# A transformer kernel on one core: the mixture layer's base matmuls first, its low-rank terms stacked, its second router joined to the output

## The reference

```python
# x: 1024 tokens x 128; W1 128x512, W2 512x128; E = 3 experts of rank R = 8
gates = softmax(x @ Rw)                                    # per token, 3 values
base  = x @ W + b
z     = einsum('bsd,edr->ebsr', x, A)                      # 3 x 8 values per token
zg    = z * gates
out   = base + (1 / 8) * einsum('ebsr,erh->bsh', zg, Bm)
...
h = relu(_mole(x, W1, b1, A1, B1, R1))
out = _mole(h, W2, b2, A2, B2, R2)
```

## Time and profile before

| what | value |
|---|---|
| runs, median (lowest to highest of 3) | 780.85 us (779.65 to 781.73) |
| span of the profiled execution | 780.1 us |
| PE busy in it | 706.0 us (90%) |
| DVE, ACT, POOL busy | 435.9, 316.3, 109.9 us |
| mixture layer, first router matmul to first expert matmul | 108.17 to 162.26 us of the span |

### The profile page before, as it was taken

One profiled execution on the slowest core, in us unless ns is written; L12 is line 12 of the kernel. 1 busy time (PEld: TensorE's weight loads), 2 busy tenths in 40 slices (PEclk: granted clock), 3 DMA queues, 4 the chain that ended last, 5 costly groups with the idle time before them and its releaser, 6 DMA issues.

```text
span 780.1 us, 9898 instructions
## 1 busy us (share of the span) xinstructions
PE 706.0 (90%) x3509; PEld 473.5 (61%) x3509; DVE 435.9 (56%) x1028; ACT 316.3 (41%) x501; POOL 109.9 (14%) x88
## 2 busy tenths in 40 slices
PE   9976999999999679999999999999977998999996
PEld 5655584878876345555555555555555885655585
DVE  5579220145575746666666666666645467534444
ACT  3044102035442345555555555555532542054441
POOL 0120030003310001111111111111132360200000
PEclk9599869699997779999999999999996998699998
DMA  3111863000004000101010101010000000000000
GB/s 79 29 44 43 243 167 80 1 1 0 1 1 134 0 1 1 41 1 42 0 41 0 41 0 42 0 41 0 0 1 1 1 1 0 1 0 1 0 1 28
DMA packets 43347, 21.62 MB, mean 28 GB/s; under 512 B 14347, under 2 KB 40469, under 8 KB 43312
## 3 DMA queue, kind: packets, MB, share of 16 engines
q1 hardware_dynamic: 43312, 21.16, 10.1%
HBM read 20.55 MB, written 0.52 MB: 27 GB/s over the span
## 4 chain that ended last, share of the span: by engine, by line
PE 54%; issue 28%; DVE 11%; POOL 5%; ACT 2%; POOLq 0%; DVEq 0%
PE ps L1347 8%; PE ps L1362 8%; PE ps L1153 6%; POOL rstd L481 5%; PE ps L1565 5%; PE ps L1581 4%; PE ps L1146 2%; PE ps L1587 2%; PE ps L1199 2%; PE ps L1456 1%; PE ps L1313 1%; PE ps L1444 1%; PE ps L1280 1%; PE ps L1322 1%; DVE z L942 1%
## 5 line engine op out<-in xcount | busy, mean ns | idle before, releaser
L1153 PE MATMUL ps<-filler 128*128 128x512 bf16 x382 | 107.2, 426 | 1.5 <-POOL filler L468 0.9
L481 POOL TENSOR_TENSOR rstd<-rv,minus_half 128x4 f32<-128x4 f32 x34 | 46.9, 1380 | 349.8 <-DVE rv L795 349.8
L952 DVE SCALAR_TENSOR_TENSOR zr<-ps,zr 128x512 fp32r<-128x512 f32 x96 | 65.1, 690 | 54.5 <-ACT zr L630 54.3
L630 ACT ACTIVATE zr<-ps 128x512 fp32r<-128x512 f32 x96 | 57.5, 599 | 69.1 <-PE ps L1347 65.1
L1456 PE MATMUL ps<-wl,z 128*128 128x128 f32 x512 | 69.2, 285 | 5.2 <-ACT z L685 5.2
L1444 PE MATMUL ps<-cf,wl 128*128 128x512 f32 x128 | 63.5, 619 | 7.0 <-ACT cf L548 7.0
L1456 PEld LDWEIGHTS ps<-wl,z 128*128 128x128 f32 x512 | 62.0, 195 | 11.6 <-ACT z L685 7.9
L1153 PEld LDWEIGHTS ps<-filler 128*128 128x128 bf16 x382 | 40.4, 108 | 43.5 <-issue 15.2
L1347 PE MATMUL ps<-zr 128*128 128x512 f32 x192 | 62.2, 406 | 1.5 <-DVE zr L928 1.5
L1110 DVE SCALAR_TENSOR_TENSOR z<-z,kc 128x512 f32<-128x512 f32 x48 | 34.7, 751 | 47.8 <-ACT z L745 47.8
L1362 PE MATMUL ps<-zr 128*128 128x512 f32 x192 | 59.4, 390 | 2.0 <-DVE zr L952 2.0
(11 more groups left out here) (249 smaller groups left out, 1180.1 us busy)
## 6 DMA issues: line engine op xcount, KB each, us to landing
wl<-in_L_attn_W SPq DMA_DIRECT2D x16, 256.0 KB
big<-in_L_cond_weight SPq DMA_DIRECT2D x32, 64.0 KB, 1.8
arena<-in_L_cond_expert_wi SPq DMA_DIRECT2D x1, 1024.0 KB, 9.1
arena<-in_L_cond_expert_wo SPq DMA_DIRECT2D x4, 256.0 KB, 5.8
big<-in_L_ffn_q_w SPq DMA_DIRECT2D x2, 512.0 KB
big<-in_L_ffn_k_w SPq DMA_DIRECT2D x2, 512.0 KB
tree_v<-in_L_ffn_v_w SPq DMA_DIRECT2D x2, 512.0 KB
arena<-in_L_cond_share_wi SPq DMA_DIRECT2D x1, 768.0 KB, 5.6
```

Source lines behind the costliest of these rows:

```text
L481: nc.gpsimd.tensor_tensor(rstd[:, half, :], rv[:, half, :], minus_half[:, :], ALU.pow).then_inc(S_["rstd"], 1)
L630: nc.scalar.activation(hidden_part(h, n, 0), ps[h][:, n % 2, :], ACT.Relu).then_inc(S_[k + "_hi"], 1)
L952: V.scalar_tensor_tensor(hidden_part(h, n, 1), ps[h][:, n % 2, :], 0.0, hidden_part(h, n, 0), ALU.max, ALU.subtract).then_inc(S_[k + "_lo" ...
L1153: T.matmul(bank, filler[:, :].to_broadcast([P, P]), filler[:, :].to_broadcast([P, HT]), start=True, stop=True)
```

## The change

First linear: after the router's matmuls (now in bank 3) PE runs six of the eight base matmuls (chunks 0 to 2 of both halves, `base_in`) without a filler, then the transposes, and then adds the low-rank terms into the same banks; chunk 3's base matmul stands just ahead of its low-rank one. Low-rank terms: `zg` holds three copies of the 25 columns side by side in blocks of 32, so that one transpose gives 96 rows. ACT's copy rounds these to fp32r; DVE then replaces rows 32 to 63 by the remainder (`low_part`, a new step with the new wait `d_zl` on PE). The weights are stacked likewise in `lora_r`: rounded, rounded, remainder. One fp32r matmul over 96 rows then gives high x high + low x high + high x low. Second linear: `w2f` carries 155 columns (128 of W2 and 27 of A2, R2), so each hidden tile is used by one matmul for both (`base_out`, into banks 0 and 1, 256 columns per tile); the low-rank terms are added later (`lora_out`). The second round goes half by half: DVE does all of half 0, then all of half 1, then both residual sums. The fillers of `turn_parts` are gone; six stand ahead of half 1's turn. The loads of B1, b1, B2, b2 are made three times (12 instead of 4); POOL clears `zg` and makes `lora_r` ahead of the experts' split. The gate vectors' softmax starts ahead of the first mixture. Ten semaphores of the set-up become two counters (`p_mm`, `p_mmc`) with the same order; their lines are left out of the diff, and so are most removed lines, which stand in the listing above.

```diff
-        ar2 = sb("ar2", [P, FC, MER + ME])
-        b1aug = sb("b1aug", [MER + 1, FF])
-        b2aug = sb("b2aug", [MER + 1, D])
+        lora_r = sb("lora_r", [3 * QUAD, FF + D], F32R)
         w1f = sb("w1f", [P, FF])
-        w2f = sb("w2f", [P, FC, D])
+        w2f = sb("w2f", [P, FC, D + MER + ME])
...
-        zg = sb("zg", [P, 2, TILES, QUAD])
-        zgt = sb("zgt", [QUAD, 2, HT])
+        zgt = sb("zgt", [3 * QUAD, 2, HT], F32R)
...
+        lora = selt[:, :, :].rearrange("p h n -> p (h n)")[:, 0:FF + D]
+        zg = [Z[h][:, 10, 0:TILES * P].rearrange("p (i r k) -> p i r k", i=TILES, r=P // QUAD) for h in HALVES]
...
+        def second_out(h):
+            return ps[h][:, 0:2, :].rearrange("p b (i n) -> p (b i) n", i=TILES // 2)
...
+                load(w2f[:, :, D + e * MR:D + (e + 1) * MR], I["L0_ffn_A2"][e].rearrange("(c p) r -> p c r", p=P), "ld_d")
             load(ar1[:, MER:MER + ME], I["L0_ffn_R1"], "ld_d")
-            load(ar2[:, :, MER:MER + ME], I["L0_ffn_R2"].rearrange("(c p) e -> p c e", p=P), "ld_d")
+            load(w2f[:, :, D + MER:D + MER + ME], I["L0_ffn_R2"].rearrange("(c p) e -> p c e", p=P), "ld_d")
+            sp.wait_ge(S_["k_mem"], 7)
+            for r in range(0, 3 * QUAD, QUAD):
+                load(lora[r:r + MER, 0:FF], I["L0_ffn_B1"].rearrange("e r n -> (e r) n"), "ld_d")
+                load(lora[r + MER:r + MER + 1, 0:FF], row("L0_ffn_b1"), "ld_d")
+                load(lora[r:r + MER, FF:], I["L0_ffn_B2"].rearrange("e r n -> (e r) n"), "ld_d")
+                load(lora[r + MER:r + MER + 1, FF:], row("L0_ffn_b2"), "ld_d")
             load(w1f[:, :], I["L0_ffn_W1"], "ld_d")
-            load(w2f[:, :, :], I["L0_ffn_W2"].rearrange("(c p) n -> p c n", p=P), "ld_d")
+            load(w2f[:, :, 0:D], I["L0_ffn_W2"].rearrange("(c p) n -> p c n", p=P), "ld_d")
...
+            for h in HALVES:
+                own.link(nc.gpsimd.memset(zg[h], 0.0))
+                nc.gpsimd.memset(zg[h][:, :, 0:3, MER:MER + 1], 1.0).then_inc(S_["d_zi"], 1)
+            pool.wait_ge(S_["ld_d"], 16 * (2 * ME + 16))
+            own.link(nc.gpsimd.tensor_copy(lora_r[:, :], lora[:, :]))
+            low = slice(2 * QUAD, 3 * QUAD)
+            nc.gpsimd.tensor_tensor(lora_r[low, :], lora[low, :], lora_r[low, :], ALU.subtract).then_inc(S_["d_w"], 1)
+            pool.wait_ge(S_["d_w"], 1)
...
             act.wait_ge(S_["p_gw"], 1)
             nc.scalar.activation(gvec[:, 1, :], gvec[:, 1, :], ACT.Exp, scale=10.0,
                                  accum_out=gred[:, 1:2]).then_inc(S_["p_gw"], 1)
+            def mixture_exp(r, h):
+                act.wait_ge(S_["d_z"], 5 + 2 * h if r else 1 + h)
+                nc.scalar.activation(logit[:, h], logit[:, h], ACT.Exp).then_inc(S_["d_e"], 1)
+            def mixture_out(r, h):
+                act.wait_ge(S_["d_zt"], 2 * r + h + 1)
+                copy(zgt[:, h], ps[h][0:3 * QUAD, 3, :], "d_ztc")
+            for h in HALVES:
+                mixture_exp(0, h)
+            for h in HALVES:
+                mixture_out(0, h)
+            for h in HALVES:
+                for c in range(FC):
+                    act.wait_ge(S_["d_hid"], h * FC + c + 1)
+                    nc.scalar.activation(z(h, c), ps[h][:, c, :], ACT.Relu).then_inc(S_["d_relu"], 1)
+            for h in HALVES:
+                mixture_exp(1, h)
+                mixture_out(1, h)
...
+            dve.wait_ge(S_["ld_gv"], 16)
+            own.link(V.tensor_reduce(gred[:, 0:1], gvec[:, 0, :], AX_X, ALU.max))
+            V.tensor_scalar(gvec[:, 1, :], gvec[:, 0, :], gred[:, 0:1], None, ALU.subtract).then_inc(S_["p_gw"], 1)
             def mixture(r):
-                zr = [ps[h][:, (1, 0)[r], :].rearrange("p (i k) -> p i k", i=TILES) for h in HALVES]
+                zr = [second_out(h)[:, :, D:] if r else ps[h][:, 3, :].rearrange("p (i k) -> p i k", i=TILES) for h in HALVES]
+                rest = slice(QUAD, 2 * QUAD)
+                def logits(h):
                     dve.wait_ge(S_[("d_r1", "d_r2")[r]], h + 1)
                     own.link(V.tensor_reduce(small[:, h, 0:TILES], zr[h][:, :, MER:MER + ME], AX_X, ALU.max))
                     V.tensor_tensor(logit[:, h], zr[h][:, :, MER:MER + ME], spread(small[:, h, 0:TILES], ME), ALU.subtract
                                     ).then_inc(S_["d_z"], 1)
+                def weighted(h):
                     dve.wait_ge(S_["d_e"], 2 * r + h + 1)
                     own.link(V.tensor_reduce(small[:, h, 4:4 + TILES], logit[:, h], AX_X, ALU.add))
                     own.link(V.reciprocal(small[:, h, 8:8 + TILES], small[:, h, 4:4 + TILES]))
                                                     spread(small[:, h, 8:8 + TILES], ME), ALU.mult, ALU.mult))
                     if r == 1:
                         dve.wait_ge(S_["d_zt"], h + 1)
-                    V.tensor_tensor(zg[:, h, :, 0:MER].rearrange("p i (e r) -> p i e r", e=ME),
-                                    zr[h][:, :, 0:MER].rearrange("p i (e r) -> p i e r", e=ME),
-                                    spread(logit[:, h], MR), ALU.mult).then_inc(S_["d_z"], 1)
-            dve.wait_ge(S_["k_mem"], 8)
+                    own.link(V.tensor_tensor(zg[h][:, :, 0, 0:MER].rearrange("p i (e r) -> p i e r", e=ME),
+                                             zr[h][:, :, 0:MER].rearrange("p i (e r) -> p i e r", e=ME),
+                                             spread(logit[:, h], MR), ALU.mult))
+                    V.tensor_copy(zg[h][:, :, 1:3, 0:MER], zg[h][:, :, 0:1, 0:MER].to_broadcast([P, TILES, 2, MER])
+                                  ).then_inc(S_["d_z"], 1)
+                def low_part(h):
+                    dve.wait_ge(S_["d_ztc"], 2 * r + h + 1)
+                    V.tensor_tensor(zgt[rest, h], ps[h][rest, 3, :], zgt[rest, h], ALU.subtract).then_inc(S_["d_zl"], 1)
+                if r == 0:
+                    for h in HALVES:
+                        logits(h)
+                    for h in HALVES:
+                        weighted(h)
+                    for h in HALVES:
+                        low_part(h)
+                else:
+                    for h in HALVES:
+                        logits(h)
+                        weighted(h)
+                        low_part(h)
+            dve.wait_ge(S_["d_zi"], 2)
...
-                residual(h, ps[h][:, 1, :], xt[1], xt[0], "d_res")
+                V.tensor_tensor(xt[0][:, h], second_out(h)[:, :, 0:D], xt[1][:, h], ALU.add).then_inc(S_["d_res"], 1)
...
-            pe.wait_ge(S_["ld_d"], 16 * (2 * ME + 8))
+            pe.wait_ge(S_["ld_d"], 16 * (2 * ME + 16))
             for h in HALVES:
                 pe.wait_ge(S_["c_out"], h + 1)
                 for i in range(TILES):
+                    ins = T.matmul(ps[h][:, 3, i * P:i * P + MER + ME], cf[:, h][:, tok(h, i)], ar1[:, :], start=True, stop=True)
                 ins.then_inc(S_["d_r1"], 1)
-            def turn_parts(r):
-                keep_warm(4, ps[0][:, 2, :])
+            def base_in(c, h):
+                T.matmul(ps[h][:, c, :], w1f[:, c * P:(c + 1) * P], cf[:, h], start=True, stop=False)
+            def turn_parts(r, h):
+                pe.wait_ge(S_["d_z"], 6 + 2 * h if r else 3 + h)
+                for i in range(TILES):
+                    ins = T.transpose(ps[h][0:3 * QUAD, 3, tok(h, i)], zg[h][:, i, 0:3].rearrange("p r k -> p (r k)"), ident)
+                ins.then_inc(S_["d_zt"], 1)
+            for c in range(FC - 1):
+                for h in HALVES:
+                    base_in(c, h)
+            for h in HALVES:
+                turn_parts(0, h)
+            pe.wait_ge(S_["d_w"], 1)
+            for h in HALVES:
+                pe.wait_ge(S_["d_zl"], h + 1)
+                for c in range(FC):
+                    if c == FC - 1:
+                        base_in(c, h)
+                    T.matmul(ps[h][:, c, :], lora_r[:, c * P:(c + 1) * P], zgt[:, h], start=False, stop=True
                              ).then_inc(S_["d_hid"], 1)
+            def base_out(h, tiles):
+                for i in tiles:
+                    for c in range(FC):
+                        ins = T.matmul(second_out(h)[:, i, 0:D + MER + ME], z(h, c)[:, tok(h, i)], w2f[:, c, :],
+                                       start=(i % 2 == 0 and c == 0), stop=False, skip_group_check=True)
+                if TILES - 1 in tiles:
+                    ins.then_inc(S_["d_r2"], 1)
+            def lora_out(h):
+                pe.wait_ge(S_["d_zl"], 2 + h + 1)
                 for i in range(TILES):
-                for i in range(TILES):
+                    ins = T.matmul(second_out(h)[:, i, 0:D], zgt[:, h, tok(h, i)], lora_r[:, FF:],
+                                   start=False, stop=True, skip_group_check=True)
                 ins.then_inc(S_["d_out"], 1)
+            pe.wait_ge(S_["d_relu"], FC)
+            base_out(0, range(TILES))
+            pe.wait_ge(S_["d_relu"], 2 * FC)
+            base_out(1, range(TILES // 2))
```

(8 more changed lines are left out.)

114 lines of the change are left out of this document (33 added, 81 removed).

## The result

The changed kernel took 755.95 us (median of 4 runs, 754.89 to 760.88), the kernel before 781.29 us beside it (779.65 to 790.66). The ratio is 0.970, with a 95% interval of 0.967 to 0.974: some 23 us faster. The forecast was 761.3 us, with a range of 758.5 to 767.0.

A forecast was written before the change was run, and what follows sets the result against it. The mixture stage was taken as bound by TensorE's work and its clock. Stage terms gave 162.26 - 142.7 = 19.6 us, so span 780.1 becomes 760.5, plus 0.75 makes 761.3 us; range 758.5 to 767.0.

The forecast's parts named there:

- The sum of the new stage: Router to first expert matmul: that matmul moves from 162.26 to 142.7 us, a gain of 19.6 us.
- six base matmuls: First linear: start near 111.6 us, 1.7 us each at low clock until 114.5, then 0.893 each, ending at 118.35.
- The wait d_zl: First linear, after the stack's transposes: TensorE waits for VectorE's low part from 119.45 to 120.45 us.
- changes of row count: First linear's low-rank and last base matmuls: four changes at 0.15 us each, 0.6 us in all.
- The joined matmul: Second linear: 155 columns at 0.294 us each, 32 taking 9.4 us; bounds 0.249 and 0.473.
- the tail: Half 1's turn to experts: grows, TensorE nearly idle from 137.85 to 142; 0.55 us added for low-clock transposes.
- Loads, GpSimd, renamed semaphores: Eight more load issues cost 2.9 us, GpSimd's split starts near 101.4; both hidden by slack, and renaming costs nothing.
- Rivals one: Mid-stage, 118.35 to 120.45: the clock falls for about 3 us, costing 1.7 us; 763.0 us, chance 0.18.
- rival four: Whole stage slower: clock stays at 1.2 GHz from 111.6 us to the experts; 784 us, chance 0.03.
- five: First linear: base does not run ahead because stack or rounded weights are late, 3 us lost; 764.3 us, chance 0.06.
- Rival two: Second linear: joined matmul costs the sum of both, 0.473 us, adding 5.7 us; 767.0 us, chance 0.08.
- Rival three: Tail stays at full clock and experts start at it: 0.55 and some 1.7 us less; 759.0 us, chance 0.10.

The follow-up runs named there:

- no_ahead: Changed kernel with the base matmuls back behind the turn, each beside its low-rank one, with four fillers; 758.70 us, ratio 0.972 to the kernel before.
- rows128: Kernel before with its 25-row low-rank operands padded with zeros to 128 rows; ratio 0.989, median 771.0 us.
- second_before: Changed kernel with the second linear put back as before, its 27-column router run separate; 765.56 us, ratio 0.982 to the kernel before.
- f32_low: Changed kernel with low-rank matmuls as plain f32 of 25 rows again, without rounding or subtraction; 770.07 us, ratio 0.988 to the kernel before.
- best_rows: best with the attention's 1-row bias matmul padded with zeros to 128 rows; 751.20 us, ratio 0.963 to the kernel before.
- before_again: Kernel before, unedited, run and profiled a second time; 780.08 us, ratio 0.999.
- best: Changed kernel with two base matmuls moved behind the transposes, no six fillers, half 0's tail beside half 1's mixture; 755.52 us, ratio 0.972 to the kernel before.
- wide_router: Kernel before with its second router's 32 matmuls widened from 27 to 128 columns, the extra ones unused; ratio 0.994, median 774.6 us.

## Why the prediction was too slow, step by step

**What bounds the kernel** was right: the stage is TensorE's work and its clock, and both moved. **The sum of the new stage** was right to 1.0 us, in part by luck, since its terms missed by 0.7 us below to 0.9 above and partly cancel. Its terms, cut as the prediction cut them:

| step | forecast us | measured us |
|---|---|---|
| router's first matmuls | 3.4 | 3.41 |
| six base matmuls | 6.75 | 7.69 |
| transposes and the new wait | 2.1 | 2.09 |
| eight low-rank, two base | 4.2 | 3.66 |
| 24 joined | 7.05 | 6.37 |
| turn, eight joined | 2.9 | 2.45 |
| four low-rank outputs, coefficients | 1.35 | 1.60 |
| six fillers | 1.35 | 1.32 |
| half 1's turn to the experts | 5.4 | 4.89 |
| sum | 34.5 | 33.5 |

- The base matmuls came out 0.9 dearer, since the clock was low for 5.0 us of them and not 2.9. At the upper clock they were priced well: in no_ahead and rows128 they read 0.86.
- The wait d_zl was forecast as 1.0 us and was 1.06. The low-rank matmuls cost about 0.23 each, near the 0.225 taken from the earlier trace rows. Most of the 0.6 us for changes of row count did not come: 96 rows next to 128 cost nothing that shows (1.09 us for a pair in no_ahead, where 0.86 + 0.225 is 1.09). That term carried the 25-row price over to another row count.
- The joined matmul was mis-sized: 0.262 us, not 0.294, and 32 x 0.032 = 1.0 us. The slope towards 512 columns was right and its end point was not. The eight matmuls of the earlier trace rows that gave 0.249 stand between matmuls of 3 rows, and about 0.2 us of their 1.99 are changes of row count; a 128-column matmul among its like costs 0.223 (rows128, second_before). From there 27 x 0.00166 more make 0.268. The base matmul's 0.893 was read from the start of a run, just behind a wait; in the midst of a run it is 0.86.
- In the tail, the clock fell only at 137.0, so the transposes cost what they did at the upper clock until then. Half 0's low-rank output read 0.59 for four, where I took 0.45.
- Loads, GpSimd, renamed semaphores: hidden as forecast. The experts' split began at 100.60 (forecast 101.4), and no engine waits for it.
- Rivals one, four and five did not come: the clock read 1.00 from 113 to 137. Rival two is excluded by 0.262. Rival three, the tail at the upper clock, came in its first part, the 0.55 us of transposes; the experts still began at the lower clock, until 140.4.

**The step that failed is what the gain was counted from.** I subtracted from the one profiled execution of the kernel before, in which the old stage took 54.1 us. It took 58.6 in the next one, when the clock fell in the first linear. Nothing in my sum allowed for that, since I read the 25-row matmuls as paying 0.16 us each for the change of rows, and as holding the clock. I named only the 27 columns as what brings it down. The prediction says so against rival four: "17 us of f32 matmuls held it". They held it in one execution and not in the next. rows128, f32_low and best_rows show in three places what few rows cost: 8 us, 14 together with the number format, and 4. What let the clock fall in the one execution and not in the other stays open.

**How much of the miss this explains.** Over all executions that the comparisons used, the kernel before averages 779.8 us (49 of them) and the changed one 757.9 (14, from 754.9 to 761.8). The mean gain is 21.9 us, where I forecast 19.55. So 2.4 of the 5.35 us are the forecast's. Of these, 1.0 is the new stage, shorter than summed, above all for the joined matmul. The remaining 1.4 are what is left over, and I put them down to the old stage, dearer on average than its first profile; its two profiles average 56.4 us, 2.3 above the 54.1. Another 1.1 us is that the median I started from, 780.85, lay above the mean, and 1.9 that the four executions of the result lay below theirs. These 3.0 us are chance. The split is rough: by the medians of the same executions (780.7 and 756.7) the gain is 24.0 us, and the forecast's share 4.4.

**The split between the halves was wrong as well.** I had 7.2 us from the first half of the stage and 12.35 from the second. The first gave 6.8 us by the first profile and 9.7 by the second (23.69 and 26.56 against 16.85 from the router's first matmul to the second router). second_before, which has the new first linear, new low-rank terms in both and no joining, is some 14 us under the kernel before; joining adds 7.2. Of the second half's 13.8 us, 6.2 came without it, where my prices had 2.4 for the low-rank outputs (eight at 0.41 less eight at 0.11).

**The range** was too narrow below. Its low end held only the tail. The lower bound of the joined matmul, which I had kept as 0.249, would have put another 1.4 us there. And the executions of one kernel differ by some 3 us to either side (754.9 to 761.8 for the changed one), for which three runs of before within 2.1 us gave too little. With both, the low end would have been near 754, and the result inside.

**The profile's own time.** The run of a profiled execution is longer than its span by 1.8 to 2.0 us in eleven of thirteen cases here (754.89 against 753.0, 758.57 against 756.7), and by 2.5 in f32_low and 2.7 in no_ahead. The profile of before, at 780.1, thus belongs to an execution of about 782.0, above all three runs shown. I had read 0.75 us as what lies around the span. It does no harm while one subtracts from the median, but it was the sign that the profile was not an average execution.

## What to carry to other kernels

Count the rows of a matmul's contraction as well as its columns: an f32 matmul of 1 or 25 rows between ones of 128 makes its neighbours dearer too, and in each of the three places here where such matmuls were padded or stacked, the time fell by about 4 us or more. Where a small matmul uses the stationary operand of a larger one, append its columns to the larger one's; it then costs some 0.04 us instead of 0.2. And before a difference of a few microseconds is read out of two profiles, ask how far two profiles of the same kernel lie apart; here one stage differed by 4.5 us with no edit at all.

## What the hardware showed that was not expected

- The granted clock fell from 1.00 to 0.50 while TensorE had no gap: in before_again after 13.00 of 13.00 us busy, in f32_low amid 25-row matmuls, in best at 81.7 us amid 1-row ones. It fell in the 1-row run in thirteen profiles of thirteen and did not in best_rows, the only one with that run padded. It held for 41 us in wide_router, where the 27 columns were filled up but the 25 rows were left. So few rows are not enough for a fall, and why the clock holds in one execution of the kernel before and falls in the next is not settled by these runs. That few-row matmuls help it to fall is what best_rows and f32_low support.
- An f32 matmul with 512 columns takes 0.86 us among its like, 1.05 beside one of 25 rows. Three of 25 rows one after the other took 0.91 each (f32_low), so what costs is the change of row count. With 128 columns 0.22, and 0.42 beside one of 1 row. With 96 rows (fp32r) beside 128 no such price shows. The load itself takes 0.18 to 0.19 us either way; in the dear cases it does not start ahead of its own matmul.
- In f32 with 128 rows and at the upper clock, a matmul of 27 columns costs 0.22 us, one of 128 columns as much, one of 155 columns 0.26 and one of 512 columns 0.86.
- Filling base work into a time at the lower clock gained nothing over fillers (no_ahead: stages of 33.2 and 33.0 us), since the work then runs at that clock (six base matmuls in 7.69 us).
